# Both at once: attention one slot ahead of the FFN, and another order of work at the beginning

## The reference

```python
xn = _layernorm(x)
local_out  = softmax(q_l @ k_l.T * scale) @ v_l                 # 1024 x 1024 scores per batch
masked     = where(scores_s >= kth, scores_s, NEG_INF)          # kth: the 102nd largest of a row's 1024
sparse_out = softmax(masked) @ v_s
mem_out    = concat([xp, softmax(xp @ bank.T) @ bank]) @ mem_out_w + mem_out_b
pred_out   = gelu((xn @ pred_in_w + b) @ pred1_w + b) @ pred2_w + b
s = concat([local_out, sparse_out, mem_out, pred_out], -1) @ warboss_w + warboss_b
g = silu(relu(xn @ w1 + b1) @ w2 + b2)                          # 512 -> 2048 -> 512
return x + s * g
```

## Time and profile before

| | |
|---|---|
| median of 3 runs | 2587.35 us |
| profiled execution: its own time | 2589.47 us |
| its span, first to last instruction | 2587.7 us |
| PE busy | 2535.0 us, 98% |
| DVE busy | 2317.5 us, 90% |
| stage 1 (PE) | 26.4 to 502.4 us |
| stage 2 | 502.4 to the end |
| mean granted clock of PE | 0.993 |

### The profile page before, as it was taken

The page is one execution under the profiler, slowest core; times in us unless marked ns, Lnnn a source line. Parts: engine busy times, 40 slices in busy tenths (PEclk is TensorE's granted clock), DMA queues, the critical chain, the costliest instruction groups (busy, mean ns, idle before and its releaser), DMA issues.

```text
span 2587.7 us, 37027 instructions
## 1 busy us (share of the span) xinstructions
PE 2535.0 (98%) x12900; PEld 2149.0 (83%) x12900; DVE 2317.5 (90%) x5194; ACT 1363.0 (53%) x2311; POOL 1118.1 (43%) x862
## 2 busy tenths in 40 slices
PE   6999999889999999999999999999999999999998
PEld 5888888778888888888888888888888888888886
DVE  7666666589999999999999999999999999999996
ACT  5777777634444444444444444444445454444443
POOL 4445554423444444444444444444444444444444
PEclk9999999989999999999999999999999999999999
DMA  6887788774566456645664566456645654565454
GB/s 217 302 306 296 294 311 305 294 267 155 196 213 217 163 196 214 214 166 196 216 215 164 196 215 214 165 197 215 214 164 196 213 210 163 196 230 200 165 201 166
DMA packets 166776, 558.60 MB, mean 216 GB/s; under 512 B 18048, under 2 KB 31040, under 8 KB 158144
## 3 DMA queue, kind: packets, MB, share of 16 engines
q1 hardware_dynamic: 166592, 556.24, 60.9%
HBM read 421.96 MB, written 134.22 MB: 215 GB/s over the span
## 4 chain that ended last, share of the span: by engine, by line
PE 94%; DVE 4%; DMA 1%; POOL 1%; ACT 0%; issue 0%; POOLq 0%; SPq 0%; ACTq 0%
PE acc L59 9%; PE acc L61 9%; PE acc L60 9%; PE hid L61 9%; PE hid L59 9%; PE hid L60 9%; PE ps L59 5%; PE ps L61 5%; PE ps L60 5%; PE o L59 5%; PE o L61 5%; PE o L60 5%; PE scores L1299 4%; PE scores L59 2%; PE scores L61 2%; PE scores L60 2%
## 5 line engine op out<-in xcount | busy, mean ns | idle before, releaser
L1052 POOL TENSOR_TENSOR h_lo<-h,h_hi 128x512 fp32r<-128x512 f32 x256 | 333.7, 1304 | 866.6 <-ACT h_hi L950 865.4
L1192 DVE MAX8 top_l<-larger 128x8 f32<-128x512 f32 x832 | 576.4, 693 | 13.2
L1212 DVE MATCH_REPLACE8 larger<-top_l,larger 128x512 f32<-128x512 f32 x768 | 521.6, 679 | 0.0
L949 ACT ACTIVATE h<-hid,small 128x512 f32<-128x512 f32 x256 | 176.5, 690 | 483.3 <-PE hid L61 483.3
L59 PE MATMUL acc<-w2s,h_hi 128*128 128x512 f32 x1024 | 412.1, 402 | 0.0
L59 PE MATMUL hid<-xnT,w 128*128 128x512 f32 x1024 | 400.3, 391 | 4.4 <-DMA w<-ffn_scratch 4.4
L61 PE MATMUL hid<-xnT,w 128*128 128x512 f32 x1024 | 400.5, 391 | 0.0
L61 PE MATMUL acc<-w2s,h_lo 128*128 128x512 f32 x1024 | 400.3, 391 | 0.0
L60 PE MATMUL acc<-w2s,h_hi 128*128 128x512 f32 x1024 | 400.2, 391 | 0.0
L60 PE MATMUL hid<-xnT,w 128*128 128x512 f32 x1024 | 400.0, 391 | 0.0
L1052 POOL TENSOR_TENSOR pT_s<-pT,pT_s 128x512 fp32r<-128x512 f32 x256 | 326.7, 1299 | 52.5 <-ACT pT_s L962 52.5
(11 more groups left out here) (175 smaller groups left out, 5593.5 us busy)
## 6 DMA issues: line engine op xcount, KB each, us to landing
w2s<-ffn_scratch SPq DMA_DIRECT2D x259, 512.0 KB, 3.9
w<-ffn_scratch SPq DMA_DIRECT2D x258, 512.0 KB, 4.2
tl<-tile_scratch SPq DMA_DIRECT2D x66, 512.0 KB, 3.9
xnT_scratch<-xnT SPq DMA_DIRECT2D x16, 2048.0 KB, 13.6
kv_scratch<-kv_out SPq DMA_DIRECT2D x32, 1024.0 KB, 5.6
tile_scratch<-tiles_out SPq DMA_DIRECT2D x16, 2048.0 KB, 8.3
xnT<-xnT_scratch SPq DMA_DIRECT2D x64, 512.0 KB, 7.0
xin<-in_L_attn_x SPq DMA_DIRECT2D x17, 1024.0 KB, 9.1
```

Of the source, the lines that this page charges most:

```text
L949: nc.scalar.activation(h32[:, c % 2, :], hid[:, :], ACT.Relu, bias=bias)
L1052: return nc.gpsimd.tensor_tensor(out_, value, hi_.bitcast(F32), ALU.subtract).then_inc(ready, 1)
L1192: l_step = count(nc.vector.max(top_l[:, own], larger[:, :]))
L1212: l_step = count(nc.vector.match_replace(larger[:, :], top_l[:, own], larger[:, :], LOWEST))
```

## The change

**Slots.** The scores of tile 0 move into stage 1. PE computes them for the sparse head after "qs" of half 14 and for the local head after "pi" of half 15 (`first_scores`), ACT makes their exponents and local probabilities in half 15, and DVE works through the 13 rounds of the search between its other work of the last two halves (`first_search`, a generator: 4 rounds in half 14, 9 in half 15). The keys, the first tiles, the first FFN weights and half 0's tokens are loaded in halves 13 to 15. Stage 2 then runs slots 1 to 63 with attention of tile m and FFN slot F = m - 1, and after them FFN slot 63 beside the rest of the last tile. `scores` is now one tensor of two PSUM banks over both stages, which leaves stage 1 six banks (`BANKS = 6`). Gates and residuals are five slots behind instead of four, `mixed` has three buffers, and the last two tiles' residuals are done by DVE. The transposes and the token load for a half 16, which nothing used, are gone.

**Beginning.** x comes in four DMAs, one a tile. ACT casts the weights of "mp" and "pi" first and DVE subtracts them; POOL subtracts the others once the first tokens are split, column block by column block, and the output weights after "qs" of half 0. Layer norm 1 moves behind the memory weights of half 0, and half 0 has an order of jobs of its own. The memory bank's projection moves behind "pi".

```diff
+FIRST_JOBS = ["mp", "pi", "ql", "ms", "p1a", "p1b", "qs", "kl", "ks", "v01", "wt", "tr0", "p2", "tr1", "mo", "tr2",
+              "tr3", "v23"]
-BANKS = 8
+BANKS = 6
...
-                sp.dma_start(xin[:, :, :], x[0, 0:HALF, :].rearrange("(t p) d -> p t d", p=P)).then_inc(x_in, 16)
+                for t in range(HTILES):
+                    sp.dma_start(xin[:, t, :], x[0, t * P:(t + 1) * P, :]).then_inc(x0_in[t], 16)
...
-                for k in range(2 * KT):
-                    pool.wait_ge(w_h, k + 1)
...
+                pool.wait_ge(xlo_ready, KT)
+                pool.wait_ge(w_h, 1 + KT)
+                for m, size in ((QL, 1), (QS, 1), (KL, 1), (KS, 1), (VL, 2)):
+                    c = slice(m * P, (m + size) * P)
+                    pool.tensor_tensor(wp_lo[:, :, c], wp[:, :, c], wp_hi[:, :, c].bitcast(F32), ALU.subtract)\
+                        .then_inc(w_split, 1)
+                for k in range(KT):
+                    pool.wait_ge(w_h, 2 + KT + k)
+                    pool.tensor_tensor(ww_lo[:, k, :], ww[:, k, :], ww_hi[:, k, :].bitcast(F32), ALU.subtract)\
+                        .then_inc(ww_split, 1)
...
                                     if first(n):
-                                        act.wait_ge(w_split, 2 * KT)
+                                        act.wait_ge(ww_split, KT)
...
+                            if (n, name) == (0, "qs"):
+                                act.wait_ge(ww_in, 16)
+                                for k in range(KT):
+                                    nc.scalar.activation(ww_hi[:, k, :], ww[:, k, :], ACT.Copy).then_inc(w_h, 1)
+                            if (n, name) == (LAST - 1, "qs"):
+                                act.wait_ge(shared.ss_done, 1)
+                                nc.scalar.activation(shared.sc(), scores[:, :], ACT.Copy, scale=SCALE)\
+                                    .then_inc(shared.sc_ready, 1)
+                            if (n, name) == (LAST, "ms"):
+                                act.wait_ge(shared.nml_ready, 1)
+                                nc.scalar.activation(shared.prob(0), scores[:, :], ACT.Exp, bias=nml[:, :], scale=SCALE,
+                                                     accum_out=sums[:, 0:1]).then_inc(shared.el_ready, 1)
+                                act.wait_ge(shared.nms_ready, 1)
+                                nc.scalar.activation(shared.prob(1), shared.sc(), ACT.Exp, bias=nms[:, 0:1])\
+                                    .then_inc(shared.es_ready, 1)
+                            if (n, name) == (LAST, "qs"):
+                                act.wait_ge(shared.invl_ready, 1)
+                                nc.scalar.activation(shared.prob(0), shared.prob(0), ACT.Copy, scale=inv[:, 0:1])\
+                                    .then_inc(shared.pl_ready, 1)
...
+                        if first(n):
+                            layer_norm(1)
...
-                load_kv(U_KL, 0)
                 load_w2(1, 1)
-                load_tl(1, 1, 1)
-                sp.wait_ge(kv_st, 16 * 4 * B)
...
+                load_tl(2, 2, 2)
+                sp.wait_ge(kv_st, 32 * HALVES)
+                load_w2(2, 2)
+                load_kv(U_VL, 0)
...
-                        if r == R_SUMS and T % HTILES == 0 and not known_first(m, 1):
-                            sums_of_half(2 * b + T // HTILES - 1)
-                        if r == R_GATE and not known_first(m, HTILES):
-                            gates(m - HTILES, T % HTILES)
+                        if r == R_SUMS and T % HTILES == 1 and not known_first(m, 5):
+                            sums_of_half((m - 5) // HTILES)
+                        if r == R_GATE and not known_first(m, 5):
+                            gates(m - 5, (m - 5) % HTILES)
...
+                for m in range(SLOTS - 2, SLOTS):
+                    t = m % HTILES
+                    dve.wait_ge(gate_ready, m + 1)
+                    nc.vector.tensor_tensor(gate[:, t, :], gate[:, t, :], mixed_of(m), ALU.mult).then_inc(last_prod, 1)
+                    dve.wait_ge(last_prod, m + 3 - SLOTS)
+                    dve.wait_ge(xr_last[m % 2], 16)
+                    nc.vector.tensor_tensor(gate[:, t, :], gate[:, t, :], residual_of(m), ALU.add).then_inc(fin_last, 1)
```

More of the change, by code:

```diff
@@ L111, in stage1 @@
     xnT = shared.xnT
+    xnT_raw, scores = shared.xnT_raw, shared.scores
     kv_st, tiles_st = shared.kv_st, shared.tiles_st
-    LAST = 2 * B - 1
+    LAST = HALVES - 1
+    ORDER = [(n, name) for n in range(HALVES) for name in jobs(n) if n < LAST or name[:2] != "tr"]
+    PLACE = {job: KT + i for i, job in enumerate(ORDER)}
     XP, PIN, WT = range(3)
@@ L403, in steps @@
                         n = 2 * b + hh
[L404 removed]
+                        for name in jobs(n):
+                            if (n, name) not in PLACE:
+                                continue
                             src = ps[:, bank(n, name), :]
@@ L615, in steps @@
                         n = 2 * b + hh
-                        for name in JOBS:
+                        for name in jobs(n):
+                            if (n, name) not in PLACE:
+                                continue
                             bk = bank(n, name)
@@ L928, in _ @@
+                for m in range(1, SLOTS + 1):
+                    slot(m)
+                for m in (SLOTS - 2, SLOTS - 1):
+                    load_x(m)
+                for m in range(SLOTS - HTILES, SLOTS):
+                    store(m)
                 for t in range(HTILES):
@@ L1040, in _ @@
+                for m in range(1, SLOTS):
+                    slot(m)
+                last = SLOTS - 1
+                C = c = HC * last
+                chunk(C, c)
                 sparse_probabilities(last, 1 + last % 2)
                 transposed(last, 0)
+                chunk(C + 1, c + 1)
                 transposed(last, 1)
-                for t in range(2):
-                    gates(last - HTILES + 1 + t, t)
+                gates(last - HTILES, last % HTILES)
+                chunk(C + 2, c + 2)
@@ L1045, in _ @@
                 head_out(last, 1)
-                for t in range(2, HTILES):
-                    gates(last - HTILES + 1 + t, t)
+                chunk(C + 3, c + 3)
+                for t in range(HTILES):
+                    gates(SLOTS - HTILES + t, t)
             @block.gpsimd
@@ L1107, in _, with slot @@
[L1107 to L1115 removed]
+                def slot(m):
+                    C = c = HC * (m - 1)
+                    chunk(C, c)
+                    transposed(m - 1, 0)
+                    chunk(C + 1, c + 1)
+                    if m % 2 == 0:
+                        transposed(m - 1, 1)
+                        chunk(C + 2, c + 2)
+                        head_out(m - 1, 1)
+                        if not known_first(m, 5):
+                            residual(m - 5)
+                    else:
+                        if not known_first(m, 5):
+                            residual(m - 5)
+                        chunk(C + 2, c + 2)
+                        transposed(m - 1, 1)
+                    chunk(C + 3, c + 3)
+                    if m % 2 == 1:
+                        head_out(m - 1, 0)
@@ L1117, in _ @@
+                for m in range(1, SLOTS + 1):
+                    slot(m)
+                residual(SLOTS - 4)
+                residual(SLOTS - 3)
             @block.vector
```

819 lines of the change are left out of this document (460 added, 359 removed).

## The result

The changed kernel takes 2607.97 us (median of 4 runs, 2606.26 to 2608.30), the kernel before, measured beside it, 2587.51: +20.5 us, a ratio of 1.0078 (95% interval 1.0065 to 1.0091). The forecast was 2596.5 in a range of 2584 to 2607: slower, as said, but by twice as much. The profiled execution took 2607.74 us, its span 2606.0 against 2587.7: +18.3 us. The other 2.2 are that the profiled execution of before stood about 2 us over its median.

The account below looks back on a forecast made before the run. PE bounds the kernel, busy 2535.0 of 2587.7 us. Terms 0.5 + 1.6 - 5.0 - 6.4 + 22 - 3.6 = +9.1 us, added to the median 2587.35, gave 2596.5 us, range 2584 to 2607.

Parts of the forecast that it names:

- the beginning: Start through half 0: first projection 6.6 us sooner, but half 0 gives most back, ending near 60; +0.5 us (-3 to +4).
- 22 - 5.0 - 6.4: Odd-slot waits +22; scores and transposes done before chunk 2 -5.0; slot 1's wait and low clock gone -6.4 us.
- the end: Behind the last FFN matmul: 12.5 us remain instead of 16.1 without PE's work; -3.6 us (-5 to -2).
- its last four operations each wait for an operation of POOL: Layer norm 1 in half 0: case costing 6 us more, half 0 ending at 63, the term then +4.
- The change of stages: Stage 1's last halves to FFN chunk 2: half 14's 1.4 us and a slightly later chunk 2; +1.6 us (-3 to +5).
- The account by DMA: Change of stages: 9 MB between half 15's key store and FFN chunk 2 take 26.9 us, setting chunk 2's start.
- The slots: Odd slots 5 to 61: moved sums delay the probabilities, 15 PE waits of 1.46 us; +22 us (+18 to +27).
- The rivals without waits: Odd slots: slack in the chain from sums to probabilities, so no waits come; 2574.5 us, chance 0.10.
- with a lower clock: Odd slots: each new wait lowers PE's clock, 15 times 2.5, 37 us more; 2634 us, chance 0.06.
- Behind chunk 2: Slot 1 and after: its 5.7 us wait and about 2.7 of half clock go, chunk 2's wait costs some; -6.4 us.
- the beginning keeps its 6.6 us: Half 0: layer norm 1 ends before POOL's splits begin, half 0 ends near 54; 2590.5 us, chance 0.12.

Follow-up runs that it names:

- e2: Changed kernel with POOL waiting for the second layer norm before it splits the output weights; 2603.40 us, 1.0065 to the kernel before.
- e3: Changed kernel with all of the old beginning put back, attention still one slot ahead with six banks; 2599.96 us, 1.0048 to the kernel before.
- e4: Changed kernel with search rounds behind the memory-output subtraction (halves 14, 15) and half 15's probabilities behind the memory output's eviction; 2606.47 us, 1.0077 to the kernel before.
- e11: e10 with the edit of e4 in the last two halves of stage 1; 2576.83 us, 0.9959 to the kernel before.
- after: The changed kernel itself, as profiled, against the kernel before; median 2607.97 us, ratio 1.0078.
- e1: Changed kernel with the local scores' maximum and inverse one search round sooner in odd slots that have the four sums; 2601.12 us, 1.0050 to the kernel before.
- e5: e1 with the second mix also one round sooner (6 instead of 7) in the same odd slots; 2584.03 us, 0.9984 to the kernel before.
- e10: Edits of e5 and e3 together, plus POOL waiting for the first normed tokens before splitting projection weights; 2577.61 us, 0.9963 to the kernel before.
- e12: e10 with the bank's projection behind the second projection, first tokens' subtractions before small weights, output-weight casts behind sparse queries; 2578.93 us, 0.9965 to the kernel before.

## Why the prediction was right in its sign and wrong in its size

By the profiled spans, forecast against measured: the beginning +0.5, +7.0; from there to chunk 2 +1.6, +6.1; from chunk 2 to the last FFN matmul, less the 9.2 us of PE's work that used to stand behind it, +10.6 (22 - 5.0 - 6.4), +8.3; the end -3.6, -3.1. Together +9.1 against +18.3. Two of the four left the bounds that they were given (+4 and +5).

- **The beginning is the step that failed.** The first projection was forecast near 20.3 and stood at 19.08: right. Then the prediction let the norm take 9.0 us with "two small operations at 1.2 instead of 0.2 beside POOL", and priced the other case as "its last four operations each wait for an operation of POOL". The earlier trace rows had the measure (1.21 for an operation on 128x4), but it was taken for two operations because POOL stopped there, and not applied to all that would stand beside POOL. Ten did, nine of them at 1.0 more each and one at 2.1; the four large ones met POOL idle. The norm took 18.6 us and ended at 54.0 instead of 47.5. POOL's other operations of half 0, 8.8 us behind the split, were not counted at all. On top came the clock: the matmuls in the 6.6 us at 0.50 cost some 3 us more, an estimate from 0.427 against 0.227 us a matmul. e2 shows the cause: with POOL idle the norm took 7.2. e3 shows the size: without the new beginning 8.0 us come back.
  The Trainium skill (SBUF — State Buffer, section "SBUF: two separate sides") puts operations of VectorE with two inputs in SBUF, beside an operation of GpSimd that reads SBUF, under the same lock as those in a two-port mode. The trace agrees: 1.19 to 1.22 for small products with two inputs, 0.16 in e2. The statistics beside POOL in the earlier trace rows (2.46) and the search's operations (0.69) took no longer. The prediction quoted only the half on the two-port mode. No run tells a shared port from another cause by which DVE waits for POOL.
- **The change of stages** was off by 4.5, the second term that was too small. The account by DMA, 26.9 us from the store of the keys to chunk 2, fits the three kernels in which PE waited for those weights: 26.1 in e4, 27.2 in e11, 27.8 in e2. In `after` the store stood at 513.12, and by that account the weights would have been there at 540.0; PE was later still, at 541.48, without a wait for them, so PE's own losses set it. The prediction took DMA's path for the longer one. Of PE's losses, GELU's split (1.8; forecast 3.4 late) and the memory output in half 15 (3.6; forecast 2.6 or more) were named. The 1.7 in half 14 and the half clock behind both were not (1.6 us lost in half 14, some 3 in the 5.9 us at 0.50 from 512.10).
- **The slots** came as forecast: 15 waits, in every fourth slot, for the probabilities, 129.16 us for four slots where 129.3 was said, clock 1.00. The term is 20.3 instead of 22; a wait is 1.29 instead of 1.46. e1 and e5 show that the order of DVE's work is the cause. The rivals without waits and with a lower clock both fall. But the row that the prediction held against the lower clock, 1.00 in 2562.40 to 2564.30, was weak. In the same trace, after 1.1 us of work and in the next idle stretch, the clock is 0.53:

```profile
2566.00:2568.00 2.00, 0.00 (x0) 0.03 (x1) 0.00 (x0) 2.00 (x5) 1.41 (x2) 0.53 0.00 0
```

  The Trainium skill's rule for that rival (TensorE: Matmul & The Clock Gate, section "A second HAM failure mode: psum-queue depth-cycling") is about frequent short idles between groups of matmuls. One wait of 1.3 us every 129 us did not bring its swing: 1.00 over 1940 us. No run has the frequent ones.
- **Behind chunk 2**, slot 1 has a wait of 0.6 instead of 5.7 and no low clock, and PE had the three groups of scores and one of transposes behind it: 8.3 - 20.3 = -12.0 against -11.4. **The end**: 13.0 us behind the last matmul against 12.5.
- **The rival "the beginning keeps its 6.6 us"** is out: the order of POOL and DVE decided it, more sharply than forecast.

What stays open: why the same wait of 1.7 us in half 14 was followed by the half clock in seven profiles and by the full clock in four, in kernels with the same code there; and whether any order keeps the 6 us of the sooner tokens. Three arrangements (e2, e10, e12) each moved the collision to another place.

## What to carry to other kernels

A chain of tiny dependent operations of DVE is a bad thing to put beside a busy POOL: each paid for most of an operation of POOL here (0.16 became 1.2), so count operations, not columns. When one link of an evenly loaded schedule is moved, look for every reader of the late engine in that slot: the one behind the first wait had only 0.5 us less at stake (0.75 against 1.29), and one round's shift of each gave all 22 us back. A limit that a trace shows (here DMA's 26 to 28 us) is a floor, and the sum needs the latest of all floors, not the one that set the time before.

## What the runs showed of the hardware

- DVE operations on 128x4 took 0.16 us with POOL idle and 1.15 to 1.22 beside its operations of 1.27 us, at times 2.3; subtractions of 512 columns took 0.69 with POOL idle and up to 2.5 beside it. Statistics, MAX8 and MATCH_REPLACE took the same beside POOL as alone. POOL lost less: its four splits took 5.04 to 5.08 beside the norm, which is four times 1.27, and 6.31 beside GELU's split in e2.
- PE's clock fell to 1.2 GHz behind a wait of 10.8 us (for 6.6 us) and behind two in a row of 1.8 and 3.6 us. Behind single waits of 1.3 us every 129 us it stayed at 2.4 GHz for 1940 us, and behind one of 1.7 us it fell in some executions for 3.3 us and in others not.
